# Four edits to an f32 layer on one core: an expert stage in one line, one GpSimd product fewer per scan period, step matmuls a period ahead, residuals in dead buffers

## The reference, cut to what matters

```python
# 1. experts: shared SwiGLU plus top-2 of 8 GELU experts, per token
shared = (silu(x @ sw1.T) * (x @ sw3.T)) @ sw2.T            # hidden 512
s = sigmoid(x @ router_w.T + (t_emb @ router_t_w.T)); top 2, gates normalised
routed = sum_e gate[e] * (gelu(x @ rw1[e].T) @ rw2[e].T)    # hidden 128 each
c = (shared + routed) / 3
# 2. state scan, once forward and once on the flipped sequence, batch 2 each
u, z = split(c @ inproj); uc = silu(conv4(u)); dt, B, C = split(uc @ xproj)
delta = softplus(dt @ dt_w + dt_b)
h_t = exp(delta_t * A) * h_(t-1) + (delta_t * uc_t) * B_t   # 512 channels x 16 states
y = (sum_n h_t C_t + uc * Dp) * silu(z); y = y @ outproj
# 3. gate between y_f and y_b, projection, residual, magnitude mask of x
# 4. soft mixture of 64 experts x 32 slots (dispatch softmax over the batch,
#    combine softmax over all slots), plus the residual
```

## Time and profile before

| | us |
|---|---|
| median of 3 runs | 1604.61 (1604.26 to 1607.12) |
| the profiled execution, its own time | 1605.49 |
| span of its trace | 1603.6 |
| PE, DVE, POOL, ACT busy | 1201.7, 1162.7, 955.8, 769.2 |
| experts, until PE's last matmul of that part | 208.5 |
| scan periods, from the first scan to the last gate | 260.5 to 1114.7 |
| mixture's last sums to the end | 1568.1 to 1603.6 |

### The profile page before, as it was taken

How to read it: one execution, slowest core, us unless ns; L and a number is a source line. 1 busy time by engine, 2 the same in 40 slices (tenths; PEclk the granted TensorE clock), 3 DMA queues, 4 the chain that set the end, 5 groups by cost and what they waited for, 6 DMA issues and landing times. The chain is left out here.

```text
span 1603.6 us, 14746 instructions
## 1 busy us (share of the span) xinstructions
PE 1201.7 (75%) x4900; PEld 670.2 (42%) x4900; DVE 1162.7 (73%) x1014; ACT 769.2 (48%) x1017; POOL 955.8 (60%) x426
## 2 busy tenths in 40 slices
PE   6899974698629887478885554444663999999997
PEld 3688831233103332123321111111232778787886
DVE  5543355899999999999999999997277554444544
ACT  4343455576636675557665535542134544333330
POOL 4420015999999999999999999995355000000000
PEclk9899996798869898679888766666885999999999
DMA  5133017322463233534323443120601230301103
GB/s 185 40 118 105 27 30 303 144 99 82 160 240 131 79 131 148 189 125 145 144 108 117 159 170 117 47 98 0 218 27 41 117 132 1 131 0 69 48 13 92
DMA packets 44415, 173.74 MB, mean 108 GB/s; under 512 B 5681, under 2 KB 10289, under 8 KB 31554
## 3 DMA queue, kind: packets, MB, share of 16 engines
q1 hardware_dynamic: 44354, 172.98, 29.3%
HBM read 138.89 MB, written 34.08 MB: 108 GB/s over the span
## 5 line engine op out<-in xcount | busy, mean ns | idle before, releaser
L1033 POOL TENSOR_TENSOR scan_dbu<-scan_rep,scan_bc 128x1024 f32<-128x1024 f32 x256 | 596.4, 2351 | 37.5 <-DMA scan_rep<-dd_rows 37.4
L973 ACT ACTIVATE scan_hs<-scan_rep,scan_neg_a 128x1024 f32<-128x1024 f32 x256 | 286.0, 1118 | 324.2 <-DVE scan_hc L1090 260.3
L1080 DVE TENSOR_TENSOR_SCAN scan_hs<-scan_hs,scan_dbu 128x1024 f32<-128x1024 f32 x176 | 402.8, 2288 | 45.5 <-POOL scan_dbu L1033 28.4
L881 PE MATMUL scan_ysum<-scan_hc,scan_sel 128*32 128x512 f32 x1024 | 177.7, 827 | 281.1 <-DVE scan_hc L1090 207.4
L1090 DVE TENSOR_TENSOR scan_hc<-scan_hs,scan_bc 128x1024 f32<-128x1024 f32 x176 | 215.2, 1223 | 5.6
L881 PEld LDWEIGHTS scan_ysum<-scan_hc,scan_sel 128*32 128x32 f32 x1024 | 37.2, 133 | 401.1 <-issue 304.5
L1080 DVE TENSOR_TENSOR_SCAN scan_hc<-scan_hs,scan_dbu 128x1024 f32<-128x1024 f32 x80 | 181.3, 2278 | 12.0 <-POOL scan_dbu L1033 11.5
L1039 POOL TENSOR_TENSOR scan_hc<-scan_hc,scan_bc 128x1024 f32<-128x1024 f32 x80 | 187.8, 2348 | 0.2 <-DVE scan_hc L1080 0.2
L806 PE MATMUL scan_pb<-scan_xin,scan_inwf 128*128 128x512 f32 x384 | 171.8, 601 | 0.0
L806 PEld LDWEIGHTS scan_pb<-scan_xin,scan_inwf 128*128 128x128 f32 x384 | 71.8, 191 | 102.4 <-issue 102.4
L32 PE MATMUL ffn_sl<-ffn_tanh_s,xm_s 128*128 128x512 f32 x384 | 106.0, 411 | 2.3 <-DVE ffn_tanh_s L1792 2.3
(11 more groups left out here) (186 smaller groups left out, 1663.0 us busy)
## 6 DMA issues: line engine op xcount, KB each, us to landing
scan_rep<-dd_rows SPq DMA_DIRECT2D x64, 1024.0 KB, 5.5
scan_bc<-bc_rows SPq DMA_DIRECT2D x32, 512.0 KB, 5.6
dd_rows<-scan_dd SPq DMA_DIRECT2D x16, 1024.0 KB, 3.9
ffn_wt<-in_ew SPq DMA_DIRECT2D x16, 1024.0 KB, 7.6
scan_inwf<-fold SPq DMA_DIRECT2D x12, 512.0 KB, 5.5
cond<-scan_bc SPq DMA_DIRECT2D x16, 256.0 KB, 3.5
scan_xin<-cond SPq DMA_DIRECT2D x4, 1024.0 KB, 8.1
y_all<-scan_yo SPq DMA_DIRECT2D x8, 512.0 KB, 3.1
```

The costliest lines, as they stand in the source:

```text
L881: mm = nc.tensor.matmul(ysum[i * D32:(i + 1) * D32, h, :], sel[:], hc[:, (s0 + i) % HCR, h * CT:(h + 1) * CT], start=False, stop=last, til ...
L973: nc.scalar.activation(hs[:, s % HSR, :], rep[:, e % REPS, 0, :], ACT.Exp, scale=neg_a[:, k % 2, NI * dc + i, r // NI:r // NI + 1]).then_i ...
L1033: nc.gpsimd.tensor_tensor(dbu[:, s % DBR, :], rep[:, e % REPS, 1, :], bc[:, j, 0, :], ALU.mult).then_inc(dbu_done, 1)
L1080: nc.vector.tensor_tensor_scan(states, hs[:, s % HSR, :], dbu[:, s % DBR, :], 0.0, ALU.mult, ALU.add).then_inc(scan_done, 1)
```

## The change

Expert stage: the units of all chunks are numbered `g = 0 ... 47` on PE, ACT and DVE, so that the next chunk's values and factors are issued before the last two projections of the chunk. `hid` is gone: the product is written over the factor in PSUM, and high and low parts are made from there. The router's matmuls (`logits`) go behind value and factor of unit 0, sw3 is loaded before the other chunks of x, and values 4, 5 and 6 with `project(2)` and `project(3)` run before `turn_gates`. ACT reads out a chunk's sum after `hidden` of unit 1 of the next chunk, DVE turns it after unit 2.

```diff
-            for c in range(NC):
-                pe.wait_ge(loaded_x[c], 16)
-                for k in range(KC):
-                    mm = nc.tensor.matmul(by_expert[c * E32:(c + 1) * E32, :], rout[:, k, :], xT[:, k, c * CT:(c + 1) * CT],
-                                          start=(k == 0), stop=(k == KC - 1), tile_position=(0, c * E32))
-            mm.then_inc(logits_done, 1)
+            def logits():
...
+            value(0)
+            factor(0)
+            logits()
+            value(1)
+            turn_logits()
+            factor(1)
+            value(2)
+            factor(2)
+            project(0)
+            value(3)
+            factor(3)
+            project(1)
+            value(4)
+            project(2)
+            value(5)
+            project(3)
+            value(6)
+            turn_gates()
+            factor(4)
+            factor(5)
+            factor(6)
+            project(4)
+            for g in range(SU + 3, NC * UNITS):
+                value(g)
+                factor(g)
+                project(g - 2)
...
             high(X0 - 1)
             high(SW1 - 1)
+            high(SW3 - 1)
             act.wait_ge(t_done, 1)
             nc.scalar.activation(t_logit[:], t_part, ACT.Copy).then_inc(t_copied, 1)
+            hidden(0)
...
-                nc.vector.tensor_tensor(hid[:, u % 2, :], act_h[:, u % 2, :], first[:, u % 3, 1, :], ALU.mult
+                nc.vector.tensor_tensor(first[:, g % 3, 1, :], act_h[:, g % 2, :], first[:, g % 3, 1, :], ALU.mult
...
-                nc.vector.tensor_tensor(hid_s[1][:, u % HB, :], hid[:, u % 2, :], hid_s[0][:, u % HB, :].bitcast(F32),
+                nc.vector.tensor_tensor(hid_s[1][:, g % HB, :], first[:, g % 3, 1, :], hid_s[0][:, g % HB, :].bitcast(F32),
...
+            product(0)
             dve.wait_ge(loaded_tri, 2 * 16)
             dve.wait_ge(probs_done, 1)
```

Scan:

```diff
 def pool_unit(s):
     r = s % UPP
-    return r % NI == 0 or r == 2 * NI + 1
+    return r % NI == 0
...
     if r == 0:
-        step = [("t", k, p + 1)] if p + 1 < DC else [("t", n, 0)] if more else []
+        step = [("t", n, 0)] if p + 1 == DC and more else [("t", 0, 1)] if (k, p) == (0, 0) else []
...
-    return (old.get((p, r), []) if done else []) + (new.get((p, r), []) if more else [])
+    step = [("t", k, p + 2)] if p + 2 < DC else [("t", n, 1)] if p + 1 == DC and more else []
+    step = [(*key, h) for key in step for h in range(HALVES)] if r == NJ - 1 else []
+    return (old.get((p, r), []) if done else []) + (new.get((p, r), []) if more else []) + step
...
-GATE_AT, EXP_AT, LN_AT = 4, 5, 5
-STEP_IN_AT = 2
+STEP_AT = (1, 2, 3)
+LATE_STEP_AT = (3, 5, 5)
+GATE_AT = 4
-ADD_AT, DU_AT = 8, 9
+POOL_STEP_AT, LATE_POOL_STEP_AT = (6, 7), (8, 9)
...
+                step_in_at, exp_at, ln_at = LATE_STEP_AT if p + 1 == DC or w == 0 else STEP_AT
...
+                add_at, du_at = LATE_POOL_STEP_AT if w % DC == DC - 1 or w == 0 else POOL_STEP_AT
```

The two halves `h` of a step matmul are issued one after the other. Mixture, its end:

```diff
-        xres = ex[:, :, :, 0:DM]
+        xres = [t[:].rearrange("p s b c -> p (s b c)")[:, m * BATCH * DM:(m + 1) * BATCH * DM]
+                .rearrange("p (b d) -> p b d", b=BATCH) for t in (lsb, ex) for m in range(MT // 2)]
...
-            sp.wait_ge(et_turned, 2 * MT * NCH)
+            sp.wait_ge(exp_done, 2 * MT * NCH)
+            sp.wait_ge(diff_done, MT * NCH)
             for m in range(MT):
-                if m >= 2:
-                    sp.wait_ge(stored[m % 2], 16 * (m // 2))
-                sp.dma_start(xres[:, m % 2], x1_rows[:, :, m, :]).then_inc(res_loaded[m % 2], 16)
...
+                if m == MT // 2:
+                    sp.wait_ge(et_turned, 2 * MT * NCH)
+                sp.dma_start(xres[m], x1_rows[:, :, m, :]).then_inc(res_loaded[m], 16)
+            for m in range(MT):
+                sp.wait_ge(res_done, m + 1)
+                sp.dma_start(out[:, m * P:(m + 1) * P, :].rearrange("b p d -> p b d"), xres[m]).then_inc(stored, 16)
+            sp.wait_ge(stored, 16 * MT)
```

More of the change, by code:

```diff
@@ L295, in _, with value @@
-            for c in range(NC):
-                chunk(c)
+            def value(g):
+                c, u = divmod(g, UNITS)
+                if g == 0:
+                    pe.wait_ge(split_done, X0)
+                    pe.wait_ge(sw1_split, 1)
+                elif u == 0:
+                    pe.wait_ge(split_done, X1 + c - 2)
+                if g == SU:
+                    pe.wait_ge(split_done, RW1 - 1)
+                wait(pe, act_done, g - 2)
+                for k in range(KC):
+                    mm = split_products(nc, first[:, g % 3, 0, :], [w[:, k, u * P:(u + 1) * P] for w in w1_s],
+                                        [x[:, k, c * CT:(c + 1) * CT] for x in x_s], k == 0, k == KC - 1)
+                mm.then_inc(value_done, 1)
@@ new lines, in factor @@
+            def factor(g):
+                c, u = divmod(g, UNITS)
+                if g == 0:
+                    pe.wait_ge(split_done, SW3 - 1)
+                if g == 2:
+                    pe.wait_ge(t_copied, 1)
+                if g == SU:
+                    pe.wait_ge(ident_done, 1)
+                    pe.wait_ge(gates_ready, 2)
+                wait(pe, hid_split, g - 2)
+                out = first[:, g % 3, 1, :]
+                if u < SU:
+                    for k in range(KC):
+                        mm = split_products(nc, out, [w[:, k, u * P:(u + 1) * P] for w in w3_s],
+                                            [x[:, k, c * CT:(c + 1) * CT] for x in x_s], k == 0, k == KC - 1)
+                else:
+                    row = c * E32 + u - SU
+                    for i in range(2):
+                        mm = nc.tensor.matmul(out, ident_s[:, row:row + 1].to_broadcast([P, P]), gates_s[:, i, :],
+                                              start=(i == 0), stop=(i == 1))
+                mm.then_inc(factor_done, 1)
@@ L440, in _ @@
                                     ).then_inc(gates_ready, 1)
-            low_hidden(0, 3)
-            def chunk(c, done=0):
-                for u in range(done, UNITS):
-                    product(c, u)
-                    if u > done or (u and not done):
-                        low_hidden(c, u - 1)
-                low_hidden(c, UNITS - 1)
-                for cc in range(KC):
-                    dve.wait_ge(second_read, KC * c + cc + 1)
-                    wait(dve, stored[1][cc], 16 * c)
-                    nc.vector.tensor_copy(rev_sb[:, cc, :], out_sb[:, cc, ::-1]).then_inc(turned_back, 1)
-            chunk(0, done=SU)
-            with dve.Fori(1, NC) as c:
-                chunk(c)
+            for g in range(SU, NC * UNITS):
+                product(g)
+                if g > SU:
+                    low_hidden(g - 1)
+                if g % UNITS == 2 and g > UNITS:
+                    turn_output(g // UNITS - 1)
+            low_hidden(NC * UNITS - 1)
+            turn_output(NC - 1)
 DIN, NST, DTR, TAPS = 512, 16, 16, 4
@@ L1545, in ffn_phase @@
         w_loaded = [sem(f"w_loaded{j}") for j in range(JT)]
[L1546 removed]
+        res_loaded = [sem(f"res_loaded{m}") for m in range(MT)]
         res_done = sem("res_done")
[L1548 removed]
+        stored = sem("stored")
         block = ctx.enter_context(nc.Block())
```

212 lines of the change are left out of this document (84 added, 128 removed).

## The result

The changed kernel takes **1577.11 us** in the median (1575.93 to 1578.25, 4 runs) against 1604.43 (1602.86 to 1607.12) of the kernel before, run beside it: a ratio of 0.9828, 95% interval 0.9811 to 0.9845. Forecast were 1576.5 us, 1566 to 1591, and faster with a chance of 0.95.

What follows compares the result with a forecast made beforehand. The prediction took POOL to bound the scan, DVE next, and PE mostly to pace the experts. Scan - 18.8, experts - 6.1 and mixture's end - 3.2 took 1605.5 to 1577.4, median 1576.5 us, range 1566 to 1591.

Steps and rivals of the forecast that it cites:

- The bound of the scan: Scan: one product from POOL to DVE makes DVE the bound, 51.64 against 53.19 us a period; period 0 gains 2.3.
- The step move: Scan: step issued a period ahead, so its matmuls no longer delay the gate in 11 of 14 periods.
- Six turns, x 0.4: Scan, six period turns: half a step matmul waits for ACT's reading, delaying `gate_out` 0 to 1 us; 0.4 each, + 2.4.
- The late gate, booked at 0.35: Scan, periods where the step stays late: `z` ends about when the gate is due, so DVE waits only 0.35 us.
- the product's 1.3: Scan, last period: already DVE's, without step instructions, it pays for the moved product, + 1.3 us.
- Rival B: Scan: ACT and PE keep DVE waiting, late gates in half the periods and worse turns, 10.8 us, 1587; chance 0.20.
- Experts, chunk 0: Experts' part: reordered start removes PE's waits up to 80.89 us, - 6.1 us, ends 0 and - 12; later chunk turns nothing.
- the router some 4.4 us more: Experts, chunk 0: the router's matmuls behind the first value and factor last 4.4 us, until 21.5.
- (C): Experts, chunk 0: PE is slow throughout, starting from a standstill; 9 us more, so 1586; chance 0.08.
- `low_hidden(0)` at 0.69: Experts, chunk 0: reading PSUM, this DVE instruction takes 0.69 us instead of 2.72, - 2.0 us.
- The mixture's end, - 3.2: Mixture's end: slots loaded early, last residual starts at 1596.9 instead of 1600.13, - 3.2 us.
- Rival D: Scan: step matmuls hold back `add_states`, period 55.4 us, total 1625, slower than before; chance 0.04.

Runs made afterwards that it cites:

- three products: The changed kernel with three POOL products a scan period instead of four, thirteen on DVE: 1599.61 us, ratio 0.9964.
- Experiments 2 and 3: Kernel before with four POOL products, step unmoved: 1602.23 us; then the new scan with the step moved but five POOL products, experts and mixture as before: 1604.31 us.
- experiment 5: Changed kernel with ACT's convolution readings one place earlier: 1573.79 us; with the late step reading one unit earlier: 1578.23 us; with both: 1577.62 us.
- experiment 7: Changed kernel with the router's matmuls ahead of the first unit again and ACT's `hidden(0)` behind the probabilities: 1575.79 us, ratio 0.9834.
- experiment 6: Changed kernel with the gated hidden units written to an SBUF tile again instead of their PSUM bank: 1582.47 us, ratio 0.9866.
- the end alone: Kernel before with only the new end of the mixture, residuals in dead buffers: 1600.79 us, ratio 0.9975.
- the product only: Kernel before with four POOL products a scan period instead of five, the step where it was: 1602.23 us, ratio 0.9985.

## Why the prediction was right, and which of its terms were not

**The bound of the scan.** Right. POOL set the period before, DVE after: 51.64 a period was forecast without disturbance, 51.73 measured; three products make it 53.01. The 14 periods, 21.7 us by the forecast, would give 14 x (53.19 - 51.73) = 20.4. Period 0 gave 1.6 of the 2.3.

**The step move.** Right in its part: "it matters by what it keeps off". Experiments 2 and 3 show it: without the move each late gate costs 2.0 to 2.6 us over the usual 0.35, where the forecast had 1.2 (1.55 less 0.35, from the mildest of the six late gates on record).

**Six turns, x 0.4.** The mechanism was right, the size was not. `gate_out` waits for PE at four of the six, by 0.72, 1.08, 0.68 and 1.08, in sum 3.56 against 2.4. The step that failed is "I take 0.4" between 0 and 1. In all six the reading ends 4.76 us before `gate_out` is due; in the four the half and `add_states` behind it take 5.24 to 5.65 us, with the granted clock at 0.50 through `add_states`, and in the other two 3.62 and 4.62, with 0.72 and 0.55. The forecast's rows gave 1.89 + 3.05 = 4.94 at most.

**The late gate, booked at 0.35.** This is the term that was wrong. In the fourths and period 0 I took `z` to end about when the gate is due. It depends on where in it PE's clock falls, and in periods 0, 3 and 7 on the late step reading ahead of it (experiment 5): the waits are 1.83, 1.26 and 2.18 in periods 0, 3 and 7, and 1.36 in the last, of which nothing was booked. Over the usual 0.35 it is 0.9 + 1.8 = 2.7 us within the 14 periods and 1.0 in the last one, which with the product's 1.3 makes its + 2.5. Rival B had this, at 7 x 1.2 us; 4 gates were late. What is left of the excess in the 14 periods (7.5 over 14 x 51.73, less 2.8 of turns within them and 2.7 of gates) are 2.0 us in pieces of up to 0.4, some of them between DVE's instructions with no wait shown, which I can't assign. The scan's gain is 12.1 in the first pair of profiles; over the five profiles with its new code (mean 840.0) and three with its old (854.6) it is 14.6, against 18.8.

**Experts, chunk 0.** The gain was larger: 10.4 in the pair, 10.5 over all profiles (five with the old part, mean 208.05; seven with the new one, mean 197.5). The step that failed: "the router some 4.4 us more (part at each clock)". It took 1.94. The forecast scaled the 7.26 us of the earlier trace rows, which it took for 16 matmuls at the lower clock. They were not: the trace has the clock at the upper level from 11.6 us on, and the loads set their pace, as in experiment 7 (x lands at 7.15, 9.77, 11.12 and 12.51, the chunks' matmuls begin at 7.19, 9.81, 11.16 and 12.55). Behind unit 0 there is no load to wait for, the four chunks run side by side, and the clock is at the upper level from 17.3. (The same 0.45 priced unit 0's twelve matmuls rightly, 5.41 us, by luck: those do come 0.43 apart.) The router ended at 19.34 instead of 21.5, PE's wait for project 0 was 1.86 instead of 4.4, and project 4 ended 2.7 us ahead of the forecast. That settles (C) the other way: PE was not slow through chunk 0, the granted clock of that window is 0.96 instead of 0.84. The 0.96 is a little too good, since the trace records no clock before 17.3, where the matmuls still come 0.43 apart and not 0.23; with 0.5 up to there it is 0.93. By the Trainium skill (TensorE: Matmul & The Clock Gate, What's actually happening) activity releases the throttle; here that worked for the change, not against it. The 3.4 us of idle up to 80.89 went as booked. Some 1.5 us more went in the later chunks, where I had booked nothing and where the waits of the old kernel make up 0.5; for the rest I have no row. A term that neither the sum nor the range had is POOL's hold on a DVE instruction of 16 columns: with it the experts end at 198.10 to 199.02, without it at 195.99 to 196.24 (last section).

**`low_hidden(0)` at 0.69.** Right, and now shown by experiment 6.

**The mixture's end, - 3.2.** Right: - 2.9 in the pair of profiles, - 4.0 alone; by the table's last column - 3.8 (mean 490.4 of five with the old end, 486.7 of nine with the new one).

**Rival D** did not come about: no undisturbed turn waits, and no period is over 53.6.

The two misses, 6.7 us in the scan and 4.3 in the experts, and a stretch that took 2.65 us less by chance, cancel to nothing. The forecast came out within a microsecond with its main mechanism right, that the bound moves from POOL to DVE and the step move keeps late gates off it, and with more luck than its terms deserved.

## What to carry to other kernels

When the bound moves from one engine to another, the waits that the first one had hidden become the price: work out what each late result will cost at the new bound, and move these along with it (here 2.6 us for the product alone, nothing for the step alone, 17.0 for both). Put work that needs several loads behind work whose inputs are there already (the router: 8.6 us first, 1.94 behind one unit). And before a difference of 0.2% is believed, run the unchanged kernel again on the same chip: the stretches that nobody touched differed here by 2 to 5 us.

## What was not expected of the hardware

**How far a disturbed DVE instruction is held.** I had taken POOL's disturbance for a lengthening by so much. The rows show a wait for the end of POOL's instruction. In the changed kernel's trace a `tensor_tensor` of 16 columns, both inputs in SBUF, took 2.15 us, from 38.86 to 41.01, where another run of the same kernel has 0.18:

```profile
38.86 2.15 DVE L459 TENSOR_TENSOR moe_rden<-moe_rden,moe_big 128x16 f32<-128x16 f32 x1
```

POOL in the same trace, from 38.59 to 40.99:

```profile
38.59 2.40 POOL L388 TENSOR_TENSOR moe_w_s<-moe_rw,moe_w_s 128x1024 fp32r<-128x1024 f32 x1 [2.60 <-ACT moe_w_s L324]
```

In experiment 6 it was a `tensor_scalar` of 16 columns, with one tensor input, 1.86 us, from 40.14 to 42.00 (the others of this size took 0.17 to 0.18):

```profile
40.14 1.86 DVE L459 TENSOR_SCALAR moe_den<-moe_den 128x16 f32<-128x16 f32 x1
```

and POOL from 39.57 to 41.97:

```profile
39.57 2.40 POOL L389 TENSOR_TENSOR moe_w_s<-moe_rw,moe_w_s 128x1024 fp32r<-128x1024 f32 x1 [1.83 <-ACT moe_w_s L325]
```

The Trainium skill (SBUF — State Buffer, Who interferes with whom) calls the shared pair of ports an exclusive lock: a DVE instruction with two SBUF inputs contends with a POOL instruction that reads SBUF, a `tensor_scalar` can contend by its two-port mode, and there whoever issues first has the pair for its whole instruction and the other is blocked. Both pairs of rows agree, within 0.03 us; whether this `tensor_scalar` ran in that mode, no row tells. The instructions of 512 columns fit too: in experiment 6 POOL's instruction ends at 28.56 and `low_hidden(0)` at 29.11, in the kernel before at 27.92 and 28.47, 0.55 us behind it both times. The scan does not contradict it: POOL is busy there for 96% of the time, and DVE's products, with `scan_hs` as the one input that lies in PSUM, keep to 1223 ns:

```profile
L1115 DVE TENSOR_TENSOR scan_hc<-scan_hs,scan_bc 128x1024 f32<-128x1024 f32 x192 | 234.9, 1223 | 6.1
```

What this does to chunk 0 hangs on some tenths of a us. In the other run of the changed kernel POOL had no instruction at that place:

```profile
38.20 0.18 DVE L459 TENSOR_TENSOR moe_rden<-moe_rden,moe_big 128x16 f32<-128x16 f32 x1
```

The weights were ready at 39.35 there and at 41.99 here, the low part that `project(3)` waits for came behind them, and the experts end at 196.24 or 198.10. All seven profiles with this experts' part and order divide so. In the four that end at 198.10 to 199.02 POOL had started 0.03 to 0.28 us before this instruction, which took 2.15 to 2.39 us; in the three that end at 195.99 to 196.24 POOL was not running, and it took 0.17 or 0.18. So one DVE instruction of 16 columns moves the kernel's first stretch by 2 to 3 us.

**The scatter of PE's clock.** It changes level at other moments in kernels whose code is the same up to there. From the experts' end to the first scan the kernel before, the end alone and the product only have the same code, and take 52.01, 49.44 and 51.49 us, with PE busy for 33.55, 30.89 and 33.33 of them and DVE for 21.59, 21.60 and 21.59. In the five profiles of the scan's new code DVE is busy for 817.0 to 817.3 us, and its waits make the difference; the mean granted clock is 0.79 in the three of 840.8 to 842.6 us and 0.80 in the two of 837.1 and 837.7. That the clock's moments are the only cause of these 5 us is not shown. For a single wait, by 1.78 us, the rows of experiment 5 show it. The five later runs of the changed kernel range from 1572.95 to 1578.77; in which stretch they differ can't be told, as only one of them has a profile.
